# A three-stage decoder layer on one core: the third stage in two parts with banks of their own, gate and up products in one bank, and a new order of steps

## The reference

```python
x = x + attn(layernorm(x))            # a: 16-head causal linear attention, phi = elu + 1
x = x + xattn(layernorm(x), ctx, ctx) # b: tanh probabilities, log ratio, softmax, W_diff, layernorm, GELU MLP 256-1024-256
x = x + ffn(layernorm(x))             # c, below
# c: 128 of 256 tokens are chosen by a router score
_, idx = top_k(x @ w_router, 128)
h = rmsnorm(x[idx], g1)
x_attn = causal_softmax_attention(h @ W_qkv.T) @ W_out.T      # 16 heads of 16
h2 = rmsnorm(x[idx] + x_attn, g2)                             # the second norm
x_ff = silu(h2 @ W1.T) * (h2 @ W2.T) @ W3.T                   # 682 columns
x[idx] = x[idx] + x_attn + x_ff
```

## Time and profile before

| | |
|---|---|
| three runs, median (lowest to highest) | 1023.78 us (1022.46 to 1026.49) |
| the profiled execution, its own time | 1024.8 us |
| its span, first to last instruction | 1022.9 us |
| busy in the span | PE 90%, weight loads 77%, DVE 70%, ACT 58%, POOL 21% |
| mean granted PE clock | 0.957 of full speed |

### The profile page before, as it was taken

One profiled execution on the slowest core, in us unless ns is written; L12 is line 12 of the kernel. 1 busy time (PEld: TensorE's weight loads), 2 busy tenths in 40 slices (PEclk: granted clock), 3 DMA queues, 4 the chain that ended last, 5 costly groups with the idle time before them and its releaser, 6 DMA issues.

```text
span 1022.9 us, 21601 instructions
## 1 busy us (share of the span) xinstructions
PE 924.6 (90%) x7488; PEld 783.7 (77%) x7488; DVE 712.7 (70%) x1653; ACT 596.5 (58%) x1565; POOL 216.9 (21%) x379
## 2 busy tenths in 40 slices
PE   3868799999999999999999999999999999987866
PEld 2656779797887879787888879797978878785734
DVE  3565767777786877777777877777777868765432
ACT  2252475756667475757666574757566674735423
POOL 0011412131222313121212213121312223131000
PEclk9566999999999999999999999999999999998968
DMA  6221000010000010010000010000100010000000
GB/s 234 69 59 31 1 23 10 12 32 11 31 10 31 10 31 0 10 31 10 31 10 31 10 31 10 22 9 10 31 10 31 10 31 21 12 2 11 1 12 11
DMA packets 20320, 25.36 MB, mean 25 GB/s; under 512 B 1472, under 2 KB 17856, under 8 KB 20288
## 3 DMA queue, kind: packets, MB, share of 16 engines
q1 hardware_dynamic: 18848, 20.66, 6.3%
q10 hardware_dynamic: 1440, 4.28, 1.3%
HBM read 20.74 MB, written 4.19 MB: 24 GB/s over the span
## 4 chain that ended last, share of the span: by engine, by line
PE 71%; DVE 14%; ACT 6%; issue 5%; POOL 2%; DMA 1%; DVEq 0%; POOLq 0%; ACTq 0%; SPq 0%
PE bank L1027 20%; PE bank L1231 8%; PE bank L1113 5%; PE bank L1035 4%; PE bank L1390 4%; PE bank L1276 3%; PE bank L1190 3%; PE bank L1198 3%; PE bank L1169 3%; PE bank L1264 2%; PE bank L1131 2%; ACT L597 2%; DVE before L919 2%; PE bank L1301 2%; PE bank L1315 2%
## 5 line engine op out<-in xcount | busy, mean ns | idle before, releaser
L634 ACT ACTIVATE w_raw_or_stage_c<-bank,c_nmax 128x128 f32<-128x128 f32 x256 | 90.3, 374 | 23.5 <-DVE c_nmax L950 23.5
L705 DVE TENSOR_TENSOR b_s_lo<-prob,b_s_hi 128x512 fp32r<-128x512 f32 x64 | 43.9, 686 | 59.7 <-ACT b_s_hi L485 59.7
L778 DVE TENSOR_TENSOR a_s<-bank,const 128x512 f32<-128x512 f32 x96 | 64.3, 686 | 29.0 <-PE bank L1113 29.0
L950 DVE TENSOR_REDUCE c_nmax<-bank 128x4 f32<-128x512 f32 x64 | 42.5, 685 | 57.6 <-PE bank L1301 57.6
L1113 PE MATMUL bank<-qT_by_parity,kT 32*128 32x256 f32 x512 | 77.2, 421 | 2.6 <-DVE a_s L778 1.4
L391 POOL TENSOR_SCALAR f_rs<-f_mv 128x2 f32<-128x2 f32 x32 | 7.2, 226 | 323.9 <-DVE f_mv L714 323.9
L669 ACT ACTIVATE w_raw_or_stage_c<-bank,c_rms_half 128x384 f32<-128x384 f32 (+1 forms) x32 | 17.5, 547 | 95.9 <-POOL c_rms_half L472 58.4
L597 ACT ACTIVATE prob<-bank,b_folded 128x256 f32<-128x256 f32 x128 | 53.7, 471 | 29.7 <-PE bank L1027 25.8
L1027 PE MATMUL bank<-b_s_hi,w_mlp_hi 128*128 128x256 f32 x256 | 58.6, 311 | 5.0 <-ACT prob L597 2.3
L1113 PEld LDWEIGHTS bank<-qT_by_parity,kT 32*128 32x128 f32 x512 | 46.3, 194 | 20.7 <-issue 11.8
L408 POOL TENSOR_TENSOR a_tr_lo<-a_norm,a_tr_hi 128x512 fp32r<-128x512 f32 x16 | 20.7, 1296 | 173.1 <-ACT a_tr_hi L485 173.1
(11 more groups left out here) (237 smaller groups left out, 2891.9 us busy)
## 6 DMA issues: line engine op xcount, KB each, us to landing
x_in<-in_x SPq DMA_DIRECT2D x16, 256.0 KB, 2.8
qc<-in_ctx SPq DMA_DIRECT2D x16, 256.0 KB, 2.9
b_f<-in_ctx_t SPq DMA_DIRECT2D x16, 256.0 KB, 3.6
out<-w_raw_or_stage_c SPq DMA_DIRECT2D x16, 256.0 KB, 2.2
w_raw_or_stage_c<-in_w ACTq DMA_DIRECT2D x4, 512.0 KB, 5.1
w_raw_or_stage_c<-in_w_gu ACTq DMA_DIRECT2D x4, 341.0 KB, 3.3
const<-in_consts SPq DMA_DIRECT2D x1, 835.0 KB, 4.8
w_raw_or_stage_c<-in_w_a SPq DMA_DIRECT2D x2, 384.0 KB, 5.8
```

The costliest lines, as they stand in the source:

```text
L634: act_in(c_e[g % 2][:, j * R:(j + 1) * R], (c1, c2)[g % 2][:, j * R:(j + 1) * R], ACT.Exp, bias=c_nmax[:, n:n + 1], accum_out=c_den[:, hea ...
L705: tt(out_, full, high.bitcast(F32), ALU.subtract).then_inc(done.sem, 1)
L778: tt(heads(A_MASKED[g % 4][:, :]), heads((a1, a2)[g % 2][:, :]), tri.unsqueeze(1).broadcast_to([P, 4, P]), ALU.mult).then_inc(a_scput.sem, 1)
L950: nc.vector.tensor_reduce(c_nmax[:, 4 * g:4 * g + 4], heads((c1, c2)[g % 2][:, :]), axis=AX.X, op=ALU.max, negate=True).then_inc(c_max.sem, 1)
```

## The change

Stage c is divided at the second norm. The first part (through `c_xo`) uses banks `c1` and `c2` alone, the second part (from `c_h2tp` to `c_done`) bank `c0` alone. `c_etp` transposes back into the bank whose scores were just read. The gated activations get a buffer of their own (`gated`), where tanh writes and both gate operations work in place; the selection matrix of the second part is copied to `sel_k` on POOL (`c_tkeep`).

The gated unit is cut in three pieces of 256, 256 and 170 columns, and for each piece gate and up columns stand side by side in the weights, so that one product writes both into `c0` (512, 512 and 340 columns). `c_gu_1` therefore waits until both gate operations of piece 0 have read `c0`, and so on; transposes of the gated rows come in two pieces of 4 and 2, the second after the low part of the first was taken; `c_ff` is one step.

Before the scatter, the finished rows are split into a high and a low part (`c_yhi` on ACT, `c_ylo` on DVE), and the scatter's two plain float32 products become four float32r products. The constants are 640 columns fewer. All steps are reordered, and the loads of weights are split at other places.

```diff
-FG = 342
+GATE = ((0, 256), (256, 256), (512, FF - 512))
...
-        act = raw[:, 2, 0:FFP]
+        act = sb("gated", [P, FFP])
...
-        GATE = ((c1, c2, 0, 3 * P), (c0, c1, 3 * P, FF - 3 * P))
-        G_BANK = (c2, c0)
+        G_PIECES = ((0, 4), (4, 2))
...
+            def c_tkeep_(b):
+                pool.wait_ge(*c_selu(b, 1))
+                if not first(b):
+                    pool.wait_ge(*c_scat(b - 1))
+                pool.sem_inc(passed.sem, 1)
+                nc.gpsimd.tensor_copy(sel_k[:, :], sel_t[:, :]).then_inc(c_tkeep.sem, 1)
...
+            def c_yhi_(b):
+                act_e.wait_ge(*c_y(b))
+                copy(flat(c_hs[0][:, :, :]), c_h2[:, :], c_yhi)
...
+            def c_ylo_(b):
+                dve.wait_ge(*c_yhi(b))
+                low(flat(c_hs[1][:, :, :]), c_h2[:, :], flat(c_hs[0][:, :, :]), c_ylo)
...
             def c_rank_(b):
                 pe.wait_ge(*c_before(b))
                 if not first(b):
-                    pe.wait_ge(*c_y(b - 1))
+                    pe.wait_ge(*c_o(b - 1))
...
-            def c_gu_1_(b):
-                gate_product(c0, 0, 1).then_inc(c_gu.sem, 1)
-
-            def c_gu_2_(b):
-                pe.wait_ge(*c_gate(b, 1))
-                gate_product(c1, 1, 1).then_inc(c_gu.sem, 1)
+            def c_gu_(j):
+                def step(b):
+                    at, n = 2 * GATE[j][0], 2 * GATE[j][1]
+                    if j == 0:
+                        weights(b, len(loads))
+                        pe.wait_ge(*c_h2hi(b))
+                        pe.wait_ge(*c_h2lo(b))
+                    else:
+                        pe.wait_ge(*c_gate(b, 2 * j))
+                    split_product(c0[:, 0:n], lambda p, k: c_hs[p][:, k, :], lambda p, k: wgu[p][:, k, at:at + n], DC) \
+                        .then_inc(c_gu.sem, 1)
+                return step
...
             def c_gtp_(j):
                 def step(b):
-                    pe.wait_ge(*c_gate(b, 2 * j + 2))
-                    for f in range(3):
-                        at = (3 * j + f) * P
-                        last = nc.tensor.transpose(G_BANK[j][:, f * R:(f + 1) * R], act[:, at:at + P], ident)
-                    last.then_inc(c_gtp.sem, 1)
-                return step
...
+                    else:
+                        pe.wait_ge(*c_gtlo(b, 1))
+                    k, n = G_PIECES[j]
+                    for f in range(n):
+                        at = (k + f) * P
+                        last = nc.tensor.transpose(c0[:, f * R:(f + 1) * R], act[:, at:at + P], ident)
+                    last.then_inc(c_gtp.sem, 1)
+                return step
+
+            def c_ff_(b):
+                pe.wait_ge(*c_gthi(b))
+                pe.wait_ge(*c_gtlo(b))
+                last = split_product(c0[:, 0:D], lambda p, k: act_t[p][:, k, :], lambda p, k: w3[p][:, k, :], FFP // P)
+                last.then_inc(c_ff.sem, 1)
 
             def c_scat_(b):
-                pe.wait_ge(*c_y(b))
+                pe.wait_ge(*c_yhi(b))
+                pe.wait_ge(*c_ylo(b))
+                pe.wait_ge(*c_tkeep(b))
                 for t in range(TT):
-                    last = mm(c2[:, t * D:(t + 1) * D], sel_t[:, t * P:(t + 1) * P], c_h2[:, :], start=True, stop=True)
+                    for part in range(2):
+                        last = mm(c0[:, t * D:(t + 1) * D], sel_k[:, t * P:(t + 1) * P], flat(c_hs[part][:, :, :]),
+                                  start=part == 0, stop=part == 1)
                 last.then_inc(c_scat.sem, 1)
```

More of the change, by code:

```diff
@@ L42 @@
 ORDER = """
[L43 to L52, removed]
@@ L53 @@
-b_dtp a_phi_k c_ht b_diff a_kout b_rstd c_sel a_state a_vput a_kput c_qk a_csum a_sput b_vq a_score_0 a_mask
-b_ratio c_selu b_rtp c_hput b_log c_v b_sid b_qb b_dput b_rput c_score_0 a_kq a_scput_0 a_den b_fd c_max_0
-a_score_1 c_qkput c_max_1 b_orstd+
+c_h2lo+ c_h2put+ a_mean c_gate_0+ a_normed c_att+ b_ghi_1+ c_xo+ b_glo_1+ b_up_2+ c_h2tp+ a_yhi+ b_down_0+
+c_h2hi+ c_gu_0+ c_w2 b_gelu_2+ b_ghi_2+ c_w0 b_up_3+ a_proj+ c_tanh_0+ b_glo_2+ c_gu_1+ c_tanh_1+ a_done+
+b_kept+ a_kept+ b_mean c_gate_1+ b_down_1+ b_glo_3+ c_h2rms+ a_ylo+ b_gelu_3+ a_rstd a_tp c_gate_2+ c_gu_2+
@@ new lines @@
+b_down_2+ b_rstd c_gtp_0+ a_tlo b_ghi_3+ b_down_3+ c_gtp_1+ b_normed b_qb c_tanh_2+ c_gtlo_0+ b_o+ c_ff+ a_q
+c_gtlo_1+ a_thi b_omean+ b_pnorm b_orstd+ c_tkeep+ c_rstd c_gthi_0+ b_tanhk c_scat+ b_onormed+ c_y+ b_done+
+c_gthi_1+ c_ylo+ c_rms1 c_mean b_tanhq c_yhi+ a_qout b_diff c_w3 c_done+ a_phi_q a_kout a_vput b_frstd b_fb2
+a_k c_normed b_log a_val a_kput b_v c_sbc b_vput a_ktp a_mask b_dput c_rscore a_phi_k b_dtp c_before c_rank
+a_state b_ratio c_ht b_rtp c_hput c_qk c_v b_rput c_sel c_qkput c_vput b_sid b_vq c_score_0 c_w4 a_score_0
@@ L654, in c_h2put_ @@
                 act_e.wait_ge(*c_xo(b))
+                if not first(b):
+                    act_e.wait_ge(*c_ylo(b - 1))
                 copy(c_h2[:, :], c2[:, 0:D], c_h2put)
@@ L1348, in c_h2tp_ @@
                 pe.wait_ge(*c_h2put(b, 1))
+                if not first(b):
+                    pe.wait_ge(*c_done(b - 1))
                 for c in range(DC):
@@ L1419, in constants @@
     c = np.zeros((P, NCONST), np.float32)
-    c[:, CONST["ident2"]] = np.stack([t[None] == n * P + p[:, None] for n in range(TT)], 1).reshape(P, -1)
-    c[:, CONST["tri_ones"]] = p[:, None] <= t[None]
-    c[:, CONST["neg_mask"]] = np.where(p[None] > p[:, None], NEG, 0.0)
+    c[:, CONST["ident"]] = p[:, None] == p[None]
+    c[:, CONST["tri_ones"]] = p[:, None] <= p[None]
     c[:, CONST["head_block"]] = p[:, None] // HD == p[None] // HD
```

134 lines of the change are left out of this document (57 added, 77 removed).

## The result

The changed kernel took 1074.35 us (median of four runs, 1069.40 to 1078.72), the kernel before beside it 1025.13 (1022.46 to 1026.79): the ratio is 1.048, between 1.043 and 1.053. Slower, as forecast, but the forecast was 1055 and its range ended at 1074. The profiled execution took 1074.5 us with a span of 1072.6.

The account below looks back on a forecast made before the run. PE was taken to bound the kernel. Thirteen rounds at +1.8 us (+23.4), the last rounds +7.2 and +5.6 and the start -5, on 1024.8, gave 1056.0 profiled, 1055 us as median; range 1030 to 1074.

Parts of the forecast that it names:

- The freed time: Savings per round from scatter, gate products, gate tail and smaller idles: 0.4 + 0.1 + 1.6 + 1.2 = 3.3 us.
- old gate tail: Transposes and products ending the former gated unit: 2.8 us of work in 4.35, so 1.6 us per round freed.
- The sum of waits: New waits of PE per round, from chain, scatter, rank and later places: 1.8 + 1.7 + 0.7 + 0.9 = 5.1 us.
- This term I hold for the surest: Said of PE's wait before the scatter, for `c_ylo` at the end of DVE's list: 1.7 us per round.
- The first rival: Only the bare chain waits, later waits partly repeat the scatter's 1.7 us: round +0.2, 1034 us; chance 0.17.
- Other additions hide: Claim that `c_tkeep` on POOL and `c_yhi` (0.37 us) run beside longer DVE work, adding nothing.
- The clock: Rival: 3 us of PE's work per round at 1.2 GHz, 1.5 us more, 1075 us in all; chance 0.09.
- PE would stand six times a round: The clock rival's ground: PE's number of stops per round, likened to early slices granted 5 to 6 tenths.
- The ends: Outside the regular rounds: last round +7.6 less 0.4, one round earlier +5.6, start -5 us.
- the chain: Stage c's second part, one chain through one bank: +1.8 us of waits per round, between 1.3 and 2.2.
- the unseen waits: Waits no row shows, at `c_ht` behind the rank and at `a_score_2`: +0.9 us per round, 0 to 1.5.
- the freed idles: PE's smaller idles, 0.64 us per round, at steps that move: up to 1.2 us saved, taken whole.

Follow-up runs that it names:

- e1: The changed kernel with the scatter moved one step back on PE, behind `a_k`; 1059.24 us, ratio 1.032.
- e17: The changed kernel with three order repairs, plus a second bank (`c2`) for the second transposes of the gated rows; 1030.77 us, ratio 1.009.
- e12: The changed kernel with `b_fb2` moved on POOL, behind `b_kept` and no longer right behind `b_frstd`; 1048.20 us, ratio 1.024.
- e7: The changed kernel with products of no use filling PE's waits before the scatter and `c_ff`; 1073.13 us, ratio 1.047.
- e9: The changed kernel with products of no use filling PE's waits before `b_htp` and `a_score_2`; 1060.48 us, ratio 1.035.

## Why the prediction was off

The direction and the places of the stops forecast were right, and the start and the end together (+6.3 for +7.8); the size was 19 us short, and the actual time lay 0.35 us over the range.

- **The freed time**: the new gate products take 0.235 us at 512 columns (two start 0.47 apart from the next two, 698.91, 699.38 and 699.85), estimated at 0.227. The 0.91 of idle in the old gate tail went.
- **The sum of waits**, forecast +5.1 per round, was made place by place. The stops came at those places (`c_ff` 1.02 for 1.15, scatter 1.47 for 1.7, rank 0.83 for 1.0, `c_ht` and `a_score_2` 0.25 and 0.54, together inside 0 to 1.5). But they are not prices: e1 and e17 took two of them away whole and got 0.6 and 0 back. "This term I hold for the surest" was right about the stop and wrong about what it is worth. The first rival ("partly those 1.7 us seen twice") had this mechanism right, with the wrong consequence: the round is 2.4 longer all the same, 0.9 of it by POOL's hold below. DVE's list from the last low part to the masks grew from 7.62 to 11.30.
- **The step that failed** is the sentence "Other additions hide", which names `c_tkeep` and `c_yhi` alone and takes POOL as "busy 50 of 220 us": POOL was taken to be free, and its order was not looked at. `b_fb2` in its new place held DVE for 0.94 us per round; e12 gives back 0.91. With it the round would have been forecast at 59.5 against 59.25. The trace before had one instance of the hold, at 86.48.
- **The clock** was a rival with 9% and a price of 20 us. It came, at 11.5 us in the rounds, on top of the forecast's waits and not in their place; the forecast itself had the middle at full clock. "PE would stand six times a round" was the wrong thing to count: e7 and e9 tie the stretches to two stops. The Trainium skill ("TensorE: Matmul & The Clock Gate", section "A second HAM failure mode: psum-queue depth-cycling") describes a kernel whose PE idles briefly between groups of products as it cycles through PSUM banks, and whose clock swings between its two levels for it. Here the trace agrees, in 7 of 13 rounds, that short stops can be enough; they stand at one place of the round and wait for DVE.
- **The ends**: start -8.7 for -5 forecast. The end +15.0 for +12.8 (7.2 + 5.6): 20.2 us from the last `c_h2tp` to the last scatter where 18.1 was worked out, part of it at half clock, and 25.1 to the end for some 22.
- **The range** was narrower than its terms. The bounds of the chain, the unseen waits and the freed idles, added up, give +0.4 to +3.4 per round, not +0.7 to +2.8; measured is +2.4 at full clock and 3.3 with the half-clock stretches. (The page's first five slices, not seven, are under nine tenths; nothing rests on it.)

Forecast 23.4 for the rounds against 43.3: 11.5 from the clock, and 31.5 from 59.25 per round, of which 12 are POOL's hold. What is left, 20, is a little under the forecast. That it comes so near is partly luck, since the terms of that sum don't add.

## What to carry to other kernels

Between two places where a queue meets another engine's result, add up that other engine's whole list before pricing any single wait: a stop taken away inside the list comes back at its end. What shortens the round is work moved out of the list, or a wait of the list's own that goes, and a list that has to wait for the queue in its turn lengthens it by that wait. When waits are moved, look at where they gather and what stands beside them: here two stops of 0.60 and 0.54 us beside the scores cost the clock where one of 1.47 elsewhere did not. And read mean durations of the same instruction in both profiles, also for an engine that is off the path: a doubled mean is a cost that no wait names.
